# Experts' weights: split once into two parts kept in DRAM and loaded by both expert stages; expert results stored unit by unit, uncleared

## What is computed

```python
def _L0_ffn_ref(hidden, router_w, router_b, sw1, sb1, sw2, sb2, rw1, rb1, rw2, rb2):
    flat = hidden.reshape(T, d)
    router_probs = jax.nn.softmax(flat @ router_w + router_b, axis=-1)
    topk_probs, topk_idx = jax.lax.top_k(router_probs, TOP_K)          # 2 of 8
    weights = jnp.zeros_like(router_probs).at[jnp.arange(T)[:, None], topk_idx].add(topk_probs)
    shared_out = jax.nn.gelu(flat @ sw1 + sb1, approximate=False) @ sw2 + sb2
    h1 = jax.nn.gelu(jnp.einsum('td,edh->teh', flat, rw1) + rb1[None], approximate=False)
    expert_out = jnp.einsum('teh,ehd->ted', h1, rw2) + rb2[None]
    return shared_out + jnp.einsum('ted,te->td', expert_out, weights)
...
x = x + _L0_attn_a_ref(_layernorm(x), ...)      # first layer: differential attention, 8 heads
x = x + _L0_ffn_ref(_layernorm(x), ...)         # second: experts ("moe_a" in the kernel)
x = x + _L0_attn_b_ref(_layernorm(x), ...)
x = x + _L0_ffn_ref(_layernorm(x), ...)         # fourth: experts ("moe_b")
x = x + _L1_attn_a_ref(...); x = x + _L1_ffn_ref(...); x = x + _L1_attn_b_ref(...); x = x + _L1_ffn_ref(...)
```

## Time and profile before

| | |
|---|---|
| median of 3 runs | 4134.59 us (4132.98 to 4138.2) |
| span of the profiled execution | 4122.5 us |
| median less span | 12.1 us |
| first layer | from 0 to 560 us of the span |
| second layer (experts) | from 560 to 1047 us, units from 741 us |
| fourth layer (experts) | from 1878 to 2363 us, units from 2059 us |
| PE busy over the span | 88% |

### The profile page before, as it was taken

The page is one execution under the profiler, slowest core; times in us unless marked ns, Lnnn a source line. Parts: engine busy times, 40 slices in busy tenths (PEclk is TensorE's granted clock), DMA queues, the critical chain, the costliest instruction groups (busy, mean ns, idle before and its releaser), DMA issues. The chain is left out here.

```text
span 4122.5 us, 60134 instructions
## 1 busy us (share of the span) xinstructions
PE 3626.3 (88%) x19193; PEld 2601.5 (63%) x19256; DVE 2877.5 (70%) x5355; ACT 1924.7 (47%) x4079; POOL 1607.9 (39%) x1485
## 2 busy tenths in 40 slices
PE   4888877999599999998799869887899799999998
PEld 3555556888588888887788735444666455554666
DVE  5777656656566666645665568886888666776898
ACT  3565644344355555544344344443344465666332
POOL 3766726444465666633644321101002444441000
PEclk8999978999899999999899989999999999999999
DMA  5999902465100000001356410001201444441000
GB/s 135 302 259 269 307 23 84 151 194 162 59 16 19 19 19 19 16 4 35 100 167 180 148 48 21 21 11 23 40 0 39 91 101 109 102 114 27 11 16 16
DMA packets 228873, 358.33 MB, mean 87 GB/s; under 512 B 36482, under 2 KB 132850, under 8 KB 221810
## 3 DMA queue, kind: packets, MB, share of 16 engines
q1 hardware_dynamic: 204038, 265.38, 22.1%
q0 software_dynamic: 24544, 89.36, 8.9%
HBM read 173.82 MB, written 172.20 MB: 84 GB/s over the span
## 5 line engine op out<-in xcount | busy, mean ns | idle before, releaser
L2894 DVE TENSOR_REDUCE ab_nmx<-banks 128x1 f32<-128x512 f32 x512 | 329.0, 684 | 136.0 <-PE banks L2681 133.8
L2825 ACT ACTIVATE ab_pt<-banks 128x512 f32<-128x512 f32 x512 | 283.0, 600 | 163.9 <-PE banks L2691 154.9
L1736 POOL TENSOR_TENSOR lb_pq<-lb_pq,lb_rr 128x512 f32<-128x512 f32 x192 | 206.2, 1077 | 305.1 <-DVE lb_rr L1597 301.8
L1462 ACT ACTIVATE lb_pq<-banks,lb_nmx 128x256 f32<-128x256 f32 x384 | 178.5, 470 | 229.4 <-DVE lb_nmx L1592 226.2
L2691 PE MATMUL banks<-ab_qT,ab_kT 128*128 128x512 f32 x512 | 252.3, 497 | 5.7 <-ACT ab_pt L2825 5.7
L358 ACT ACTIVATE da_pt<-banks 128x512 f32<-128x512 f32 (+1 forms) x384 | 179.3, 537 | 124.9 <-PE banks L270 120.6
L1592 DVE TENSOR_REDUCE lb_nmx<-banks 128x2 f32<-128x512 f32 x192 | 131.1, 683 | 148.0 <-PE banks L1314 146.8
L2681 PE MATMUL banks<-ab_kT,ab_qT 128*128 128x512 f32 x512 | 208.1, 410 | 21.1 <-DVE ab_nmx L2894 14.6
L285 PE MATMUL banks<-da_pt,da_vx 128*64 128x512 f32 (+3 forms) x1024 | 165.0, 467 | 35.3 <-POOL da_pt L578 31.8
L2465 PE MATMUL banks<-w_f_dT,f_hT 128*128 128x256 f32 x768 | 178.1, 382 | 4.0 <-ACT f_hT L2511 4.0
L576 POOL TENSOR_TENSOR da_pt<-da_pt,w_da_tri 128x384 f32<-128x384 f32 x128 | 148.0, 1157 | 85.7 <-ACT da_pt L358 85.6
(11 more groups left out here) (538 smaller groups left out, 11146.5 us busy)
## 6 DMA issues: line engine op xcount, KB each, us to landing
moe_xs<-zero SPq DMA_DIRECT2D x71, 512.0 KB, 11.8
moe_ys<-zero SPq DMA_DIRECT2D x71, 512.0 KB, 11.8
moe_a_w_raw<-in_moe_w SPq DMA_DIRECT2D x48, 512.0 KB, 3.9
moe_b_w_raw<-in_moe_w SPq DMA_DIRECT2D x48, 512.0 KB, 4.0
da_spill<-da_hi SPq DMA_DIRECT2D x128, 128.0 KB, 2.4
ab_spill<-ab_hi SPq DMA_DIRECT2D x128, 128.0 KB, 2.4
ab_qT<-ab_spill POOLq DMA_DIRECT2D x32, 392.0 KB, 5.7
ab_kT<-ab_spill POOLq DMA_DIRECT2D x32, 392.0 KB, 5.3
```

What stands on the lines that cost most here:

```text
L1462: nc.scalar.activation(pq[:, n % RING, t, :], ps[:, S_BANK + n % 2, 2 * P * t:2 * P * t + 2 * P], ACT.Exp, bias=nmx[:, n % RING, t:t + 1], ...
L1736: nc.gpsimd.tensor_tensor(pq[:, n % RING, :, :], pq[:, n % RING, :, :], bcast(rr[:, n % RING, :], 2, 2 * P), ALU.mult).then_inc(s_p, 1)
L2825: nc.scalar.activation(pt[:, s % RING, :], ps[:, EXP_BANK + s % 3, :], ACT.Exp, scale=AB_D ** -0.5).then_inc(s_e, 1)
L2894: nc.vector.tensor_reduce(nmx[:, g % 2, col:col + 1], ps[:, MAX_BANK + n % 3, :], op=ALU.max, axis=AX.X, negate=True).then_inc(s_mx, 1)
```

## The change

In the first layer, all expert weights are split once. `expert_pieces` cuts them into 36 pieces of 128x512 (256 KB). Per piece SP loads the raw piece, ACT casts the hi part, DVE subtracts the lo part, SP writes both parts to the DRAM tensor `moe_split`. Batch 0 takes 2 pieces, batches 1 to 6 take 5 each, batch 7 takes 4; piece j of a batch stands at ACT's slot -8+2j and at DVE's slot -7+2j of the batch. `moe_ys` is no longer cleared; it holds the units' results one after another, 23x512 rows, and the places of each token's two results are worked out anew from the units' table (`result_places`, on DVE, once per stage). Clears fall from 142 to 71.

In the expert stages ACT's and POOL's splitting goes. SP loads hi and lo part of each weight directly into the buffers that PE reads. These loads wait for the last reader of the buffer: the first weights for the Gelu of unit i+1 (as before), the second weights for the down product W of unit i, `s_y`.

```diff
+    pieces_of = [2] + [5] * (B - 2)
+    pieces_of.append(len(pieces) - sum(pieces_of))
+    for b in range(B):
+        for j in range(pieces_of[b]):
+            scalar_jobs.setdefault(NH * b - 8 + 2 * j, []).append(("whi", b, first_piece[b] + j))
+            vector_jobs.setdefault(NH * b - 7 + 2 * j, []).append(("wlo", b, first_piece[b] + j))
...
+                def load_piece(n):
+                    if n >= 3:
+                        sp.wait_ge(s_piece_lo, n - 2)
...
+                    sp.dma_start(dst, src).then_inc(s_piece[n % 3], 16)
+                def keep_piece(n):
+                    sp.wait_ge(s_piece_lo, n + 1)
+                    for part, of in enumerate((piece_hi, piece_lo)):
+                        sp.dma_start(pieces[n][1 + part], of[:, n % 2, :].bitcast(F32)).then_inc(s_kept[n % 2], 16)
...
+                    if b == 0:
+                        load_tables(sp)
+                        for n in range(3):
+                            load_piece(n)
+                    for n in range(first_piece[b], first_piece[b] + pieces_of[b]):
+                        keep_piece(n)
+                        if n + 3 < len(pieces):
+                            load_piece(n + 3)
                     if b:
                         beside(sp, b - 1, B - 1)
-                    else:
-                        load_tables(sp)
...
+                def high_piece(n):
+                    act.wait_ge(s_piece[n % 3], 16 * (n // 3 + 1))
+                    if n >= 2:
+                        act.wait_ge(s_kept[n % 2], 32 * (n // 2))
+                    nc.scalar.copy(piece_hi[:, n % 2, :], piece_raw[:, n % 3, :]).then_inc(s_piece_hi, 1)
...
                 def load_w1(l):
-                    if l >= 1:
-                        sp.wait_ge(s_w1lo, l)
                     if l >= 2:
                         sp.wait_ge(s_g, HCH * (number[loads[l - 2][2]] + 1))
                     e = expert_of(l)
-                    sp.dma_start(w1_raw[:, :, :], a["moe_w1"][e, :, :].rearrange("(c p) n -> p c n", p=P)).then_inc(s_w1, 16)
...
+                    for part in range(2):
+                        sp.dma_start(w1_parts[part][:, l % 2, :, :].bitcast(F32),
+                                     w["moe_split"][0, e, part, :, :].rearrange("p (c n) -> p c n", c=KC)).then_inc(s_w1[l % 2], 16)
...
                 def load_w2(l):
-                    if l >= 1:
-                        sp.wait_ge(s_w2lo, l)
+                    if l >= 2:
+                        sp.wait_ge(s_y, 2 * (number[loads[l - 2][2]] + 1))
                     e = expert_of(l)
-                    sp.dma_start(w2_raw[:, :, :], a["moe_w2"][e, :, :].rearrange("(m p) n -> p m n", p=P)).then_inc(s_w2, 16)
+                    for part in range(2):
+                        sp.dma_start(w2_parts[part][:, l % 2, :, :].bitcast(F32),
+                                     w["moe_split"][1, e, part, :, :].rearrange("p (m n) -> p m n", m=HCH)).then_inc(s_w2[l % 2], 16)
...
-                    sp.dma_start(rows_of(ys, entry(1, u, ROWS - UNIT)), y[:, :, :]).then_inc(s_stored[u % 2], 16)
+                    sp.dma_start(ys[u * UNIT:(u + 1) * UNIT, :].rearrange("(t p) c -> p t c", p=P),
+                                 y[:, :, :]).then_inc(s_stored[u % 2], 16)
...
-                def high_w1(l):
...
-                def high_w2(l):
...
+                def result_places():
+                    nc.vector.tensor_tensor(base[:, :], ends[:, :], count[:, :], ALU.subtract)
...
+                    nc.vector.tensor_tensor(taken[:, :, :], bcast(w["moe_iota"][:, :], 1, B * NT * TOPK),
+                                            bcast(experts_of, 2, NE), ALU.is_equal)
+                    dve.drain()
+                    nc.vector.tensor_tensor(taken[:, :, :], taken[:, :, :], bcast(base[:, :], 1, B * NT * TOPK), ALU.mult)
+                    dve.drain()
+                    nc.vector.reduce_sum(experts_of, taken[:, :, :], axis=AX.X)
...
-                def low_w(l, parts, raw, done, ready):
...
         def clear_regions(sp, part=0, parts=1):
...
-            for k in range(part * 2 * blocks // parts, (part + 1) * 2 * blocks // parts):
-                rows = (w["moe_xs"], w["moe_ys"])[k // blocks][k % blocks * UNIT:(k % blocks + 1) * UNIT, :]
+            for k in range(part * blocks // parts, (part + 1) * blocks // parts):
+                rows = w["moe_xs"][k * UNIT:(k + 1) * UNIT, :]
```

More of the change, by code:

```diff
@@ L140, in product3, with diff_attention @@
     return done
-def diff_attention(core, w, a, spill, beside, s_x, load_rows, load_tables):
+def diff_attention(core, w, a, spill, beside, s_x, load_rows, load_tables, pieces):
     nc, ps = core.nc, core.ps
@@ L165, in diff_attention @@
     scalar_table = [(-37, "row", 0), (-21, "rms", 0), (27, "std", 0)]
+    pieces_of = [2] + [5] * (B - 2)
+    pieces_of.append(len(pieces) - sum(pieces_of))
+    first_piece = [sum(pieces_of[:b]) for b in range(B)]
     pool_table = [(-29, "xhi", 0), (-26, "square", 0), (-25, "square", 1), (-24, "square", 2), (-23, "square", 3),
@@ L220, in diff_attention @@
         s_stack = [sem(f"stack{i}") for i in range(CHUNKS)]
+        s_piece = [sem(f"piece{i}") for i in range(3)]
+        s_piece_hi, s_piece_lo = sem("piece_hi"), sem("piece_lo")
+        s_kept = [sem(f"kept{i}") for i in range(2)]
         s_odd = sem("odd_filled")
@@ L249, in _ @@
                                              src[64 * par:64 * par + 64, n % 2, :].bitcast(F32)).then_inc(s_spill[i], 16)
+                    if b == 0:
[6 more added lines that the diff above has]
+                            load_piece(n + 3)
                     if b:
                         beside(sp, b - 1, B - 1)
-                    else:
-                        load_tables(sp)
+                for i in range(2):
+                    sp.wait_ge(s_kept[i], 32 * (len(pieces) // 2))
             @block.tensor
@@ L435, in _ @@
                     for kind, b, i in scalar_jobs.get(s, ()):
-                        if kind != "row" or b:
+                        if kind == "whi":
+                            high_piece(i)
+                        elif kind != "row" or b:
                             root(kind, b)
@@ L630, with expert_pieces @@
 ROWS = SPARE + SPARES * UNIT
+PIECE = 512
+def expert_pieces(a, split):
+    pieces = []
+    for e in range(NE + 1):
+        for c in range(KC):
+            cols = slice(c * PIECE, (c + 1) * PIECE)
+            pieces.append((a["moe_w1"][e, c * P:(c + 1) * P, :], split[0, e, 0, :, cols], split[0, e, 1, :, cols]))
+        for c in range(HCH // 2):
+            cols = slice(c * PIECE, (c + 1) * PIECE)
+            rows = a["moe_w2"][e, 2 * c * P:2 * (c + 1) * P, :].rearrange("(m p) n -> p m n", p=P)
+            pieces.append((rows, split[1, e, 0, :, cols], split[1, e, 1, :, cols]))
+    return pieces
 class Choice:
@@ L921, in hidden @@
                 def hidden(i):
+                    l = load_of[i]
+                    if loads[l][1] == i:
+                        act.wait_ge(s_w1[l % 2], 48 * (l // 2 + 1))
                     for m in range(HCH):
@@ L944, in _ @@
                 for i in range(-3, N):
-                    if i + 2 in load_of and loads[load_of[i + 2]][1] == i + 2:
-                        high_w1(load_of[i + 2])
-                    if i + 1 in load_of and loads[load_of[i + 1]][1] == i + 1:
-                        high_w2(load_of[i + 1])
                     if i + 1 in routed:
@@ L1047, in units @@
                     dve.drain().then_inc(s_table, 1)
+                def result_places():
+                    nc.vector.tensor_tensor(base[:, :], ends[:, :], count[:, :], ALU.subtract)
+                    dve.drain()
+                    nc.vector.scalar_tensor_tensor(base[:, :], base[:, :], float(UNIT), w["moe_region"][:, :],
+                                                   ALU.mult, ALU.subtract)
+                    experts_of = idf[:, :, :, :].rearrange("p b t k -> p (b t k)")
+                    rows = placef[:, :, :, :].rearrange("p b t k -> p (b t k)")
+                    nc.vector.tensor_tensor(taken[:, :, :], bcast(w["moe_iota"][:, :], 1, B * NT * TOPK),
+                                            bcast(experts_of, 2, NE), ALU.is_equal)
+                    dve.drain()
+                    nc.vector.tensor_tensor(taken[:, :, :], taken[:, :, :], bcast(base[:, :], 1, B * NT * TOPK), ALU.mult)
+                    dve.drain()
+                    nc.vector.reduce_sum(experts_of, taken[:, :, :], axis=AX.X)
+                    dve.drain()
+                    nc.vector.tensor_tensor(rows, rows, experts_of, ALU.add)
+                    dve.drain()
+                    for k in range(2):
+                        dve.wait_ge(s_scatter[k], per_batch * B // 2)
+                    nc.vector.tensor_copy(place[:, :, :, :].rearrange("p b t k -> p (b t k)"), rows)
+                    dve.drain()
                 def split_hidden(i, m):
@@ L1108, in _ @@
                         low_x(i + 2)
```

(10 more changed lines are left out.)

77 lines of the change are left out of this document (43 added, 34 removed).

## The result

| | before | after |
|---|---|---|
| median | 4133.78 us (4 runs, 4129.58 to 4138.2) | 4345.37 us (4 runs, 4343.58 to 4347.95) |
| ratio | | 1.0517, 95% interval 1.0503 to 1.0531 |
| span of the profiled execution | 4122.5 us | 4343.3 us |

The account below looks back on a forecast made before the run. It took weights, their split and the Gelu to bound the units, the engine-to-engine chain the first layer. Start 5, boundaries 24, pieces 2, units 17, rest -2 gave +46 on 4122.5, plus 12.1: 4181 us; range 4122 to 4230.

Parts of the forecast that it names:

- The two signs named for this: Expert units, profile after: PE's wait for the first Gelu gone; its transposes R wait about 1.4 us for the rows.
- The third, a clock of 1.00: Expert units, profile after: the stretch of 20 units keeps a granted clock of 1.00.
- D = 0.79 + 3.5 + 1.5 + 1.5 = 7.3: Expert units: us from the end of W(i) until the rows of i+3 land; cycle 14.1, +17 us over 42 cycles.
- The two steps of 1.5: Expert units, inside D: 1.5 us each for two more 512 KB transfers, lo part and rows, behind the first weight load.
- its rival with late rows: Expert units: rows land later still, D 8.5, units +67 instead of +17, total 4231 us; chance 0.12.
- the forecast's far end of 15.3: Expert units: the cycle in us from above, with D about 8.5, +67 us.
- The estimate that the prediction works out from the Trainium skill: Expert units: 2.0 us plus bytes at 436 GB/s; 1.57 MB land after 5.6 us, D 6.4, term -21 us.
- The bound of the gain: Expert units: removing the splitting alone brings a unit from 13.7 to PE's 12.7 us, -42 us over 42 cycles.
- The boundaries of the first layer: ACT stands about 7.7 us for a spill behind clears; 4 us for each of six boundaries, +24 us (0 to +39).
- The rival "caught up": First layer: boundary stalls are caught up or clears go through sooner, the 24 us fall out, 4157 us; chance 0.08.
- The start: First layer: ACT's fourth q/k copy stands behind the cast of piece 0, first root at 75 us, +5 us (4 to 6).
- The pieces themselves: First layer: 36 casts on ACT and 36 subtractions on DVE, mostly covered by waits, +2 us; uncovered +25.

## Why the prediction was wrong, step by step

In the span the change cost 175 us more than forecast: some 107 in the two expert stages, 60 in the first layer, the rest elsewhere.

**The units: right mechanism, one term mis-sized and one missing.** The two signs named for this came: PE's wait for the first Gelu is gone, and R waits for the rows. The third, a clock of 1.00, did not. The step "D = 0.79 + 3.5 + 1.5 + 1.5 = 7.3" put the rows' landing down to what is ahead of them. The issue times came out (2.46 us from W's end to the rows' issue, against 2.56). The two steps of 1.5 did not: they were 1.9 and 2.4 in the unit shown, and the landing was 5.8 us after issue instead of 4.7. Of this, 0.8 us came from the store of `y` that SP issues 1 us behind the rows: with it moved away the steps are 1.7 and 1.5. The prediction named the store only as a reason for its rival with late rows; the change itself takes the table read out from in front of it, and that brings it closer (0.98 us behind the rows, 1.89 before). The trace of before had a warning that the single transfers of the earlier trace rows don't show: with one weight load ahead of them and the store 1.9 us behind, its rows landed 5.0 us after issue (the median of 17 from 780 to 1014 us, 4.4 to 5.9), later than the 4.7 that the sum gave them behind two. With D at 8.3 the sum alone would have given 15.1, near the forecast's far end of 15.3.

The other part was no term at all. I read the clock at 1.00 in the rows of before and wrote that nothing was to be won there; I didn't ask what the new wait of PE would lose there. The rows of before had the hint: the granted clock was 0.93 in the first layer and 1.00 in the units, and a wait of 1.08 us did not move it. What 2.9 us would do no row told, and a bound should have taken W at the lower level for it. Runs: 1.5 us in a unit where it falls, 46 us on the whole. The estimate that the prediction works out from the Trainium skill ("DMA: Bandwidth & Descriptors", Anatomy of one DMA — SWDGE (gpsimd) path) would have made D shorter, 6.4 us. The measurement went the other way, to 8.3.

**The bound of the gain.** "PE's own 12.7 us" was read from PE's busy time. It is 12.1 us when nothing waits (rows ahead of the weights), so the removal of the splitting was worth 1.6 us a unit, not 1.0. Busy time of a stretch with small waits inside holds some of them: in U a matmul's record lasts 0.39 us while the next starts 0.23 us later, so the start of each wait is counted as busy. At the wait of 1.08 us the matmul before it started 1.47 us earlier than the one behind it, so 1.24 us were lost:

```profile
855.60 0.39 PE L138 MATMUL banks<-moe_a_x_hi,moe_a_w_lo 128*128 128x512 f32 x1
857.07 0.50 PE L138 MATMUL banks<-moe_a_x_hi,moe_a_w_hi 128*128 128x512 f32 x1 [1.08 <-ACT moe_a_h_raw L927]
```

**The boundaries of the first layer: right place, right wait, wrong price.** ACT stood 9.4 us on average for 7.7 forecast. The step that failed is the next one: I subtracted chunk 3's old wait (4.7 us late instead of 7.7) and let the batch catch up to 4. A batch lost 13 us. While ACT stood, PE, DVE and POOL stood too for most of it (0.00 busy in 8 us), so little could be caught up. ACT's waits for the pieces' stores came on top, 3 us a batch (18.4 us in 6), and the low clock came behind the standstill. The rival "caught up" rested on the exponentials' 110 us of waiting; that is time in which ACT waits for PE, and it gives nothing where PE waits for ACT. That the spread clears bring a batch back to 64 us shows the cause; how the 13 us divide among wait, pieces and clock was not separated.

**The start.** +9.0 us for +5: SP issued the load of piece 0 at 70.27 us, not 68.4, and it landed after 5.4 us, not 3. Transfers of POOL that read the spills back were under way; that these slowed it, no run tests.

**The pieces themselves.** +2 was taken, with +25 as the end; 17 us is what is left when no wait for a piece's store is. Rest and tails were small, as forecast. The +4 us of the rest is within what the runs show for the same code there, 1759 to 1772 us, and the third layer took 831.7 to 832.7 in the other runs.

## What to carry to other kernels

A wait put into a queue that also issues another engine's input makes that input as late as the wait: move the urgent transfer ahead of the wait before anything is reckoned, and price it with what is issued behind it too. TensorE that will newly stand still can lose its clock as well as the time, so the work behind the stand is to be priced at the lower level as its far end. Long runs of transfers that nobody waits for belong between the transfers that somebody waits for, a few at a time: with ten in a row, their place only chose which wait was long.

## What the runs showed of the hardware

- A transfer was slowed by one that came later on the same queue: the rows landed 5.8 us after issue with a 512 KB store issued 1 us behind them, 5.0 us without (medians of 16 and 15). The Trainium skill ("DMA: Bandwidth & Descriptors", Queues, rings and completion order) says that each DMA engine takes descriptors in the order of its ring, but that a later one may finish its write before an earlier one. The 0.8 us fit the second half of this; which resource the two transfers shared, no run shows.
- After 2.8 us of standing PE's next matmuls of 256 columns started 0.21 us apart, then 0.12 (1.2 and 2.4 GHz). Standing of the same length did not always do it. In the changed kernel W began at the lower level in 35 of 43 units (after 1.9 to 3.7 us) and not in 8 (after 1.7 to 3.2); with the store moved away it did in 16 of 43 (after 1.9 to 2.7). After 1.08 us the matmuls did not slow.
